# Ten groups of tiles in place of nine, early keys in banks of their own, MLP weights prepared on VectorE, 33 loads, a new order

## The chip, the core and the metric

One core of one Trainium2 chip runs the whole kernel. The metric is device time in microseconds (us), lower is better. The profile shows the engines TensorE (PE; its weight loads PEld), VectorE (DVE), ScalarE (ACT), GpSimd (POOL) and SyncE (SP, which here only issues transfers).

## What is computed

A gated block of cross attention and a small quantised MLP, over 32 blocks ("tiles") of 128 rows by D = 128. S = 128 queries and S2 = 120 keys in each tile, hidden width 512.

```python
def _proj(x, W1, b1, W2, b2):
    h = jnp.einsum('bsd,od->bso', x, W1) + b1
    return jnp.einsum('bsd,od->bso', h, W2) + b2
# attention
qp, kp = _proj(q, W1, b1, W2, b2), _proj(k, W1, b1, W2, b2)
qk = jnp.einsum('bqd,bkd->bqk', qp, kp) * scale + mask
attn = jax.nn.softmax(qk, axis=-1)
attn_out = jnp.einsum('bqk,bkd->bqd', attn, v1)
# MLP: inputs, weights and biases rounded and clipped to 8 bits
h = relu(fixed_quant(einsum('bsi,oi->bso', fq(x), fq(w1)) + fq(b1)))
ffn_out = einsum('bsi,oi->bso', h, fq(w2)) + fq(b2)
# block
x = x + tanh(g_xattn[0]) * attn_out(_layernorm(x), ctx, ctx, mask, ...)
x = x + tanh(g_ffn[0]) * ffn_out(_layernorm(x), ...)
```

## The kernel before

The 32 tiles are cut into nine groups, `TILES = [2, 4, 4, 4, 4, 4, 4, 4, 2]`. Every group g goes through the same stages, each a function of that name on one engine:

- VectorE `stats1` takes mean and variance of x; GpSimd `roots` takes the inverse roots for the batches of groups that `ROOTS` lists; `normalise_pool` and `normalise_dve` share the normalised tiles.
- TensorE `transpose_x`, ScalarE `copy_xT` to SBUF. TensorE `project_keys` multiplies the group's keys by one folded matrix `Mk` (made at the start by `fold_mm1`, `fold_cp1`, `fold_mm2`, `fold_cp2` on TensorE and VectorE), ScalarE `copy_keys`. Then TensorE `scores`.
- VectorE `row_maxima` adds the (negated) mask and takes the maxima, ScalarE `exponentials`, TensorE `transpose_probs`, ScalarE `copy_probsT`, TensorE `attend` (times v), VectorE `residual`.
- VectorE `stats2`, GpSimd `roots`, `quantise_pool` or `quantise_dve`, TensorE `transpose_xq`, ScalarE `copy_xqT`, TensorE `hidden` (four chunks c of 128 hidden units, each in a PSUM bank `bank_H[c]`), `relu` for each chunk on ScalarE (`RELU_ON_ACT` says how many) or VectorE (`relu_dve`), TensorE `mlp_out`, VectorE `result`, and SP stores the group.

The weights of the MLP arrive as load `w`. ScalarE `scale_weights` rounds all 1028 columns of them to 8 bits (`mp_8`, line 528), and makes `w1_q` of them (line 532); GpSimd `widen_weights` makes `w2_q` and the biases. ScalarE also negates the mask (517) and makes a bf16 identity (513). `fold_base` on TensorE, ScalarE `copy_base` and VectorE `split_base` prepare a constant that `mlp_out` adds.

PSUM: `bank_T` takes both the transposed x and the projected keys in turn, so that each waits until ScalarE has copied the other; only group 0's keys go to `bank_H[0]`. SBUF buffers rotate in rings of four (`RING`). `keep_warm` puts matmuls of a zero matrix between the others ("fillers", line 379): 30 at the opening, and then 22, 9, 8, 5 and 5.

Each engine runs its steps in the order of the numbers in the table `DUE` (name and group), and waits on semaphores for its inputs. The 29 entries of `LOADS` are each one transfer on SP, but for the first on ScalarE's queue.

## Time and profile before

| | |
|---|---|
| median of 3 runs | 64.2 us (64.16 to 64.68) |
| profiled execution | 63.99 us, span 61.9 us |
| TensorE clock granted, mean | 0.998 |
| busy: PE / DVE / ACT / POOL | 57.4 / 50.8 / 49.5 / 44.6 us |
| share of the span | 93 / 82 / 80 / 72% |
| transfers | 9.08 MB, mean 147 GB/s |

The span is the time from the first to the last instruction of the profiled execution; its whole time is 2.1 us longer. Busy time is the union of an engine's instructions; a busy TensorE is not at its peak. The chain of waits follows, back from the last instruction, what released each; the timeline lists instructions in order of time, and in brackets how long the engine had been idle before and what it waited for.

### The profile page before, as it was taken

How to read it: one execution, taken by the hardware profiler on the slowest of the kernel's cores; microseconds unless marked ns; L12 is line 12 of the kernel's file. 1: busy time of each engine (PE TensorE's matmuls, PEld its weight loads, DVE VectorE, ACT ScalarE, POOL GpSimd, SP SyncE). 2: the span in 40 equal slices, each digit the busy share in tenths (PEclk: the TensorE clock that was granted, in tenths of full speed). 3: DMA queues.
4: the chain of work that ended last, by engine and by line, in shares of the span. 5: the costliest groups of instructions: out<-in, count | busy, mean ns of one | idle time of the engine just before them, and what ended most of it. 6: DMA issues, size and time to landing. Idle time of an engine off the chain costs nothing.

```text
span 61.9 us, 1729 instructions
## 1 busy us (share of the span) xinstructions
PE 57.4 (93%) x530; PEld 46.1 (74%) x530; DVE 50.8 (82%) x214; ACT 49.5 (80%) x137; POOL 44.6 (72%) x91
## 2 busy tenths in 40 slices
PE   3999999999999999999999999999999999989720
PEld 3999966676897888876987698798978685738310
DVE  4899919988978989979969979989988999973730
ACT  0800288979979899999999999999999896968700
POOL 5968899998989899989899999559339139170000
PEclk9999999999999999999999999999999999999999
DMA  0799999999999500002000400040040040404042
GB/s 0 207 324 345 309 370 396 404 375 386 382 390 376 185 16 5 0 0 85 0 11 0 164 5 0 5 169 11 0 169 0 0 169 11 167 3 169 0 169 85
DMA packets 5482, 9.08 MB, mean 147 GB/s; under 512 B 609, under 2 KB 2658, under 8 KB 5474
## 3 DMA queue, kind: packets, MB, share of 16 engines
q1 hardware_dynamic: 5328, 8.85, 40.2%
q10 hardware_dynamic: 146, 0.13, 0.7%
q8 instruction: 4, 0.07, 0.4%
q14 instruction: 4, 0.03, 0.1%
HBM read 6.88 MB, written 2.10 MB: 145 GB/s over the span
## 4 chain that ended last, share of the span: by engine, by line
PE 82%; POOL 5%; issue 4%; DVE 3%; ACT 1%; POOLq 1%; DVEq 0%
PE bank_A L451 12%; PE bank_S L435 12%; PE bank_O L492 10%; PE bank_T L413 10%; PE bank_H L379 9%; PE bank_H L477 8%; PE bank_A L444 6%; PE bank_T L426 6%; PE bank_O L487 3%; PE bank_H L466 3%; POOL rs L344 3%; POOL xq L362 2%; DVE y_sb L704 2%; ACT pr L559 1%; POOLq L123 1%
## 5 line engine op out<-in xcount | busy, mean ns | idle before, releaser
L344 POOL TENSOR_TENSOR rs<-ve,half 128x4 f32<-128x4 f32 (+2 forms) x17 | 16.6, 979 | 8.7 <-DVE nm L611 6.3
L586 ACT ACTIVATE h<-bank_H,fb_q 128x512 int8<-128x512 f32 (+1 forms) x27 | 16.3, 654 | 1.5 <-PE bank_H L477 1.5
L362 POOL TENSOR_SCALAR xq<-feed_sb,nm,rs 128x128 int8<-128x128 f32 x29 | 12.6, 451 | 0.9 <-POOL rs L344 0.2
L559 ACT ACTIVATE pr<-sc,mn 128x120 f32<-128x120 f32 x32 | 12.3, 400 | 0.2 <-DVE mn L656 0.2
L606 DVE BATCH_NORM_STATS2 st<-feed_sb 128x6 f32<-128x256 f32 x32 | 12.2, 417 | 0.0
L352 POOL TENSOR_SCALAR xn<-feed_sb,nm,rs 128x128 f32<-128x128 f32 x26 | 11.3, 448 | 0.4
L668 DVE SCALAR_TENSOR_TENSOR feed_sb<-bank_A,rec,feed_sb 128x128 f32<-128x128 f32 x32 | 9.1, 345 | 1.9 <-issue 1.7
L435 PEld LDWEIGHTS bank_S<-kpT,xaT 128*128 128x128 f32 x64 | 8.2, 191 | 2.0 <-issue 1.3
L492 PE MATMUL bank_O<-w_q,h 128*128 128x128 bf16 x128 | 9.0, 220 | 0.0
L451 PE MATMUL bank_A<-feed_sb,prT 120*128 120x128 f32 x64 | 8.9, 279 | 0.0
L656 DVE CUSTOM_DVE_ANT_0 sc<-bank_S,mask_neg 128x120 f32<-128x120 f32 x32 | 7.1, 277 | 2.1 <-PE bank_S L435 2.1
L435 PE MATMUL bank_S<-kpT,xaT 128*128 128x120 f32 x64 | 8.7, 276 | 0.0
L704 DVE SCALAR_TENSOR_TENSOR y_sb<-bank_O,tg_out,feed_sb 128x512 f32<-128x512 f32 (+1 forms) x9 | 6.2, 690 | 2.8 <-PE bank_O L492 2.2
L551 ACT ACTIVATE xaT<-bank_T 128x512 f32<-128x512 f32 (+1 forms) x9 | 5.0, 551 | 4.4 <-PE bank_T L426 4.3
L477 PE MATMUL bank_H<-xqT,w_q 128*128 128x512 bf16 (+1 forms) x36 | 8.4, 356 | 0.0
L451 PEld LDWEIGHTS bank_A<-feed_sb,prT 120*128 120x128 f32 x64 | 8.0, 191 | 0.6 <-ACT prT L568 0.4
L492 PEld LDWEIGHTS bank_O<-w_q,h 128*128 128x128 bf16 x128 | 7.2, 98 | 1.2
L379 PE MATMUL bank_H<-zeros_h 128*128 128x128 bf16 x79 | 6.7, 249 | 1.0 <-POOL zeros_h L324 1.0
L413 PE MATMUL bank_T<-feed_sb,Mk 128*128 128x480 f32 (+1 forms) x16 | 7.5, 549 | 0.0
L379 PEld LDWEIGHTS bank_H<-zeros_h 128*128 128x128 bf16 x79 | 6.2, 117 | 1.0 <-POOL zeros_h L324 1.0
L559 ACT ACTIVATION_READ_ACCUMULATOR pr<-sc,mn 128x1 f32 x32 | 6.6, 205 | 0.0
L568 ACT ACTIVATE prT<-bank_A,tg 120x512 f32<-120x512 f32 (+1 forms) x9 | 5.8, 639 | 0.5 <-PE bank_A L444 0.2
...
## 6 DMA issues: line engine op xcount, KB each, us to landing
...
```

Source lines behind the costliest of these rows:

```text
L344: nc.gpsimd.tensor_tensor(rs[:, cols], ve[:, cols], half[:, 0:cols.stop - cols.start], ALU.pow).then_inc(rs_done, 1)
L352: nc.gpsimd.tensor_scalar(xn[g % RING][:, tile(j)], x_of(g, j), nm1[:, of(g, j, 1)], rs[:, root_cols(1, g, j)], ALU.add, ALU.mult).then_in ...
L362: nc.gpsimd.tensor_scalar(low_byte(xq16[g % RING], tile(j)), x_of(g, j), nm2[:, of(g, j, 1)], rs[:, root_cols(2, g, j)], ALU.add, ALU.mult ...
L379: nc.tensor.matmul(bank_H[3][:, 0:P], zeros_h[:, :], zeros_h[:, :], start=True, stop=True)
L413: nc.tensor.matmul(bank_of_keys(g)[:, cols(g, K)], Mk[:, :], fed(f"k{g}"), start=True, stop=True).then_inc(kp_ready, 1)
L435: mm = nc.tensor.matmul(bank_S[:, j * K:(j + 1) * K], xaT[g % RING][:, tile(j)], kpT[g % RING][:, j * K:(j + 1) * K], start=True, stop=True)
L451: mm = nc.tensor.matmul(bank_A[:, tile(j)], prT[g % RING][:, tile(j)], v_of(g, j), start=True, stop=True)
L477: nc.tensor.matmul(bank_H[c][:, cols(g)], w1_q[:, c * P:(c + 1) * P], xqT[g % RING][:, cols(g)], start=True, stop=True).then_inc(h_ready, 1)
L492: mm = nc.tensor.matmul(bank_O[:, tile(j)], h16[g % RING][:, at].bitcast(BF16), w2_q[:, c * D:(c + 1) * D], start=False, stop=(j == TILES[ ...
L559: nc.scalar.activation(pr[i][:, j, :], sc[i][:, j, :], ACT.Exp, scale=-1.0, bias=mn[:, of(g, j, 1)], accum_out=den[:, of(g, j, 1)]).then_i ...
L586: nc.scalar.activation(low_byte(h16[g % RING], hcols(c, g)), bank_H[c][:, cols(g)], ACT.Relu, bias=fb1_q[:, c:c + 1]).then_inc(h_act[c], 1)
L606: nc.vector.bn_stats(both, pair).then_inc(st_done, 1)
```

## The change

- `TILES` becomes `[2, 2, 4, 4, 4, 4, 4, 4, 2, 2]`: ten groups; `ROOTS` has 20 batches for 17, and no batch joins two groups any more.
- Keys of the first four groups go to `bank_H[0]`, `[1]`, `[2]`, `[0]` and no longer share `bank_T` with x (`KEYS_AHEAD = 4`). Keys in SBUF rotate in five buffers, the MLP's three kinds in three.
- The rounding of the weights, `w1_q` and the negated mask move from ScalarE to VectorE; the bf16 identity moves to GpSimd's start; the bias row stays on ScalarE (`round_bias`).
- The shares move: x tiles normalised on VectorE from 6 to 5, quantised there from 3 to 2, hidden chunks from 9 to 12. One 1024-column fill of `h16` less on VectorE.
- Fillers behind the opening: 22, 8, 2, 3 in place of 22, 9, 8, 5, 5. 33 loads for 29, of the same bytes.
- All of `DUE` is new, and so the order on each engine.

```diff
-TILES = [2, 4, 4, 4, 4, 4, 4, 4, 2]
+TILES = [2, 2, 4, 4, 4, 4, 4, 4, 2, 2]
...
+KEY_RING = 5
+MLP_RING = 3
+KEYS_AHEAD = 4
+XN_ON_POOL = [2, 1, 2, 3, 4, 3, 4, 4, 2, 2]
+XQ_ON_POOL = [2, 2, 4, 4, 4, 4, 4, 4, 1, 1]
+RELU_ON_ACT = [2, 3, 3, 2, 3, 3, 3, 3, 3, 3]
+HBYTES_DVE = 1
+LOADS = ['a', 'x0', 'x1', 'x2', 'k0', 'm', 'k1', 'x3', 'k2', 'x4', 'w', 'x5', 'k3', 'v0', 'v1', 'k4', 'x6', 'x9',
+ 'v5', 'x8', 'k5', 'v2', 'v4', 'x7', 'v3', 'v6', 'v9', 'k6', 'v8', 'v7', 'k7', 'k9', 'k8']
...
-FILLERS = [22, 9, 8, 5, 5]
+FILLERS = [22, 8, 2, 3]
...
-            return bank_H[0] if g == 0 else bank_T
+            return bank_H[g % 3] if g < KEYS_AHEAD else bank_T
...
+            pool.wait_ge(ident_up, 1)
+            nc.gpsimd.tensor_copy(ident_h[:, :], ident[:, :]).then_inc(ident_h_up, 1)
...
             def project_keys(g):
-                if g == 0:
-                    pe.wait_ge(fold_cp, 5)
-                else:
+                if g < 3:
+                    pe.wait_ge(fold_cp, 5 if g == 0 else 6)
+                elif g < KEYS_AHEAD:
+                    pe.wait_ge(kp_out, g - 2)
+                if g >= KEYS_AHEAD:
                     pe.wait_ge(xT_out, g)
...
             def transpose_x(g):
                 if g == 0:
                     pe.wait_ge(ident_up, 1)
+                elif g < KEYS_AHEAD:
+                    pe.wait_ge(xT_out, g)
                 else:
                     pe.wait_ge(kp_out, g + 1)
...
-                    pe.wait_ge(kp_out, 1)
+                    pe.wait_ge(kp_out, KEYS_AHEAD)
...
-            def scale_weights():
-
-                wait_block(act, "w")
-                nc.scalar.activation(mp_8[:, :], mp_sb, ACT.Copy, scale=W_SCALE).then_inc(quant8, 1)
+            def round_bias():
                 act.wait_ge(row_in, 16)
...
-                nc.scalar.activation(w1_q[:, :], mp_8[:, 0:C * P], ACT.Copy, scale=1.0 / W_SCALE).then_inc(w1_up, 1)
...
+            def negate_mask():
+                wait_block(dve, "m")
+                nc.vector.tensor_scalar(mask_neg[:, :], mask_sb, -1.0, None, ALU.mult).then_inc(mask_up, 1)
+
+            def round_weights():
+                wait_block(dve, "w")
+                nc.vector.tensor_scalar(mp_8[:, :], mp_sb, W_SCALE, None, ALU.mult).then_inc(quant8, 1)
+
+            def widen_w1():
+                dve.wait_ge(quant8, 1)
+                nc.vector.tensor_scalar(w1_q[:, :], mp_8[:, 0:C * P], 1.0 / W_SCALE, None, ALU.mult).then_inc(w1_up, 1)
```

TensorE at the start, behind the 30 opening fillers. `Wc` is the folded weight in the making, `Mk` in a row's input marks a projection of keys, `ident,xn` a transpose of normalised x, `zeros_h` fillers. Before:

```order
L386 MATMUL bank_H<-feed_sb 128x129
L379 MATMUL bank_H<-zeros_h 128x128 x22
L390 MATMUL bank_H<-Wc 128x128
L391 MATMUL bank_H<-bc,Wc 128x1
L396 MATMUL bank_O<-row_sb,ones 128x2
L426 MATMUL bank_T<-ident,xn 128x128 x2
L379 MATMUL bank_H<-zeros_h 128x128 x9
L413 MATMUL bank_H<-feed_sb,Mk 128x240
L413 MATMUL bank_T<-feed_sb,Mk 128x480
L435 MATMUL bank_S<-kpT,xaT 128x120 x2
L379 MATMUL bank_H<-zeros_h 128x128 x8
```

Now:

```order
L392 MATMUL bank_H<-feed_sb 128x129
L385 MATMUL bank_H<-zeros_h 128x128 x22
L436 MATMUL bank_T<-ident,xn 128x128 x2
L396 MATMUL bank_H<-Wc 128x128
L397 MATMUL bank_H<-bc,Wc 128x1
L385 MATMUL bank_H<-zeros_h 128x128 x8
L421 MATMUL bank_H<-feed_sb,Mk 128x240
L436 MATMUL bank_T<-ident,xn 128x128 x2
L402 MATMUL bank_O<-row_sb,ones 128x2
L421 MATMUL bank_H<-feed_sb,Mk 128x240
L445 MATMUL bank_S<-kpT,xaT 128x120 x2
L436 MATMUL bank_T<-ident,xn 128x128 x4
```

Group 0's transposes (now line 436) stand ahead of the second fold (`Wc`), the gates' matmul (line 402, `row_sb,ones`) behind group 1's transposes, and group 1's keys and tiles are of two instead of four.

VectorE around the row maxima (`sc,mn<-bank_S`) of group 1. Before, from group 0's reciprocal on:

```order
L661 RECIPROCAL rec<-den 128x2
L622 TENSOR_SCALAR xn<-feed_sb,st,rs 128x128 x2
L606 BN_STATS st<-feed_sb 128x6 x2
L609 TENSOR_SCALAR ve<-st 128x4
L611 TENSOR_SCALAR nm<-st 128x4
L656 ISA sc,mn<-bank_S,mask_neg 128x120
L656 ISA mn 128x1
```

Now, from the statistics (`BN_STATS`) of group 4 on:

```order
L603 BN_STATS st<-feed_sb 128x6 x2
L606 TENSOR_SCALAR ve<-st 128x4
L608 TENSOR_SCALAR nm<-st 128x4
L670 RECIPROCAL rec<-den 128x2
L619 TENSOR_SCALAR xn<-feed_sb,st,rs 128x128
L646 TENSOR_SCALAR mp<-feed_sb 128x1028
L665 ISA sc,mn<-bank_S,mask_neg 128x120
L665 ISA mn 128x1
```

The rounding of the weights (line 646) stands directly ahead of group 1's row maxima.

TensorE at the end: `xqT,w_q` is `hidden`, `ident_h,xq` is `transpose_xq`, `base_h,units_h` begins an `mlp_out`. Before, from the output of group 6 on:

```order
L492 MATMUL bank_O<-w_q,h_2 128x128 x16
L477 MATMUL bank_H<-xqT,w_q 128x512 x4
L466 MATMUL bank_H<-ident_h,xq_0 128x128 x2
L487 MATMUL bank_O<-base_h,units_h 128x128 x4
L492 MATMUL bank_O<-w_q,h_3 128x128 x16
L477 MATMUL bank_H<-xqT,w_q 128x256 x4
L487 MATMUL bank_O<-base_h,units_h 128x128 x2
L492 MATMUL bank_O<-w_q,h_0 128x128 x8
```

Now, likewise from the output of group 6 on:

```order
L497 MATMUL bank_O<-base_h,units_h 128x128 x4
L502 MATMUL bank_O<-w_q,h_0 128x128 x16
L476 MATMUL bank_H<-ident_h,xq_2 128x128 x2
L487 MATMUL bank_H<-xqT,w_q 128x256 x4
L497 MATMUL bank_O<-base_h,units_h 128x128 x4
L502 MATMUL bank_O<-w_q,h_1 128x128 x16
L476 MATMUL bank_H<-ident_h,xq_0 128x128 x2
L487 MATMUL bank_H<-xqT,w_q 128x256 x4
L497 MATMUL bank_O<-base_h,units_h 128x128 x2
L502 MATMUL bank_O<-w_q,h_2 128x128 x8
L497 MATMUL bank_O<-base_h,units_h 128x128 x2
L502 MATMUL bank_O<-w_q,h_0 128x128 x8
```

Before, an output of each group stands ahead of the next group's `hidden`; now `hidden` of groups 7, 8 and 9 each stand ahead of the output of the group before.

## Rows read from the trace of the kernel before

**Rows 1.** Chain of waits, one period of a four-tile group: start, length (us), what

```profile
30.61 0.44 PE bank_T L426 x4
31.05 0.89 PE bank_A L451 x8
31.94 0.33 PE bank_O L487 x4
32.27 1.00 PE bank_O L492 x16
33.27 0.86 PE bank_H L477 x4
34.13 0.81 PE bank_T L413 x2
34.94 0.44 PE bank_A L444 x4
35.38 0.89 PE bank_S L435 x8
36.26 0.22 PE bank_H L466 x4
```

**Rows 2.** Chain of waits: the opening, the base, and at 24.58 us

```profile
0.97 3.14 PE bank_H L379 x30
...
4.39 1.23 PE bank_H L379 x22
...
6.09 0.31 PE bank_O L396 x2
...
13.86 0.34 PE bank_O L404 x4
14.20 0.17 PE bank_O L405
...
24.58 0.44 PE bank_A L444 x4
```

**Rows 3.** Busy time by stretch: from:to, us, each engine's busy us (instructions), PEclk, DMA

```profile
4.00:20.00 16.00, 15.91 (x132) 12.53 (x131) 13.49 (x70) 11.54 (x39) 14.36 (x27) 1.00 1.03 370
20.00:50.00 30.00, 30.00 (x280) 24.99 (x278) 27.11 (x122) 29.17 (x84) 23.62 (x44) 1.00 0.12 44
50.00:61.90 11.90, 8.47 (x95) 5.56 (x93) 7.39 (x19) 7.26 (x15) 3.46 (x6) 0.99 0.27 101
```

**Rows 4.** Timeline of TensorE at the end: start, length (us), engine, line, operation

```profile
54.49 1.04 PE L477 MATMUL bank_H<-xqT,w_q 128*128 128x512 bf16 x4
```

**Rows 5.** Timeline of ScalarE at the end

```profile
54.92 1.84 ACT L586 ACTIVATE h<-bank_H,fb_q 128x512 int8<-128x512 f32 x3 [0.48 <-PE bank_H L477]
...
57.59 1.21 ACT L586 ACTIVATE h<-bank_H,fb_q 128x256 int8<-128x256 f32 x3 [0.56 <-PE bank_H L477]
```

**Rows 6.** Timeline of VectorE, first row maxima and last result

```profile
9.27 0.28 DVE L656 CUSTOM_DVE_ANT_0 sc<-bank_S,mask_neg 128x120 f32<-128x120 f32 x1 [1.26 <-PE bank_S L435]
...
59.28 0.48 DVE L704 SCALAR_TENSOR_TENSOR y_sb<-bank_O,tg_out,feed_sb 128x256 f32<-128x256 f32 x1 [0.66 <-PE bank_O L492]
```

**Rows 7.** Groups of instructions by shape: line, operation, count, busy us, mean ns

```profile
L695 DVE TENSOR_SCALAR h<-bank_H,fb_q 128x512 int8<-128x512 f32 x6 | 4.5, 748 | 0.1
...
L600 DVE MEMSET h<- 128x1024 f32 x2 | 1.8, 912 | 0.3 <-issue 0.3
...
L695 DVE TENSOR_SCALAR h<-bank_H,fb_q 128x256 int8<-128x256 f32 x3 | 1.4, 472 | 0.0
...
L528 ACT ACTIVATE mp<-feed_sb 128x1028 int8<-128x1028 f32 x1 | 1.0, 1047 | 0.0
...
L635 DVE TENSOR_SCALAR Wc<-Wc,lift 128x128 f32<-128x128 f32 x1 | 0.3, 287 | 0.0
...
L639 DVE TENSOR_SCALAR Mk<-bank_H 128x128 f32<-128x128 f32 x1 | 0.3, 278 | 0.0
```

**Rows 8.** Timeline of GpSimd, its first root

```profile
4.72 0.74 POOL L344 TENSOR_TENSOR rs<-ve,half 128x2 f32<-128x2 f32 x1 [0.62 <-DVE nm L611]
```

More of the change, by code:

```diff
@@ new lines @@
+    transpose_x=[573, 758, 896, 1133, 1751, 2169, 2593, 3026, 3890, 4317],
+    fold_mm2=[622],
+    project_keys=[727, 811, 1030, 1221, 1458, 1909, 2333, 2736, 3459, 3999],
+    spread_gates=[789],
+    scores=[849, 987, 1345, 1584, 1984, 2395, 2939, 3373, 4031, 4411],
+    transpose_probs=[1082, 1441, 1680, 2087, 2501, 2901, 3305, 3962, 4463, 4780],
+    attend=[1272, 1540, 1821, 2229, 2648, 3069, 3726, 4111, 4624, 4936],
+    fold_base=[1717],
+    transpose_xq=[1789, 2317, 2878, 3344, 3704, 4084, 4485, 4800, 5183, 5418],
@@ new lines @@
+    hidden=[2125, 2545, 3158, 3491, 3816, 4333, 4668, 4980, 5263, 5498],
+    mlp_out=[2788, 3234, 3576, 4199, 4512, 4824, 5055, 5305, 5536, 5675],
+    copy_xT=[652, 833, 1042, 1329, 1820, 2248, 2668, 3308, 3953, 4368],
+    copy_keys=[799, 883, 1199, 1379, 1675, 2090, 2513, 2940, 3578, 4201],
+    gate=[917],
+    round_bias=[949],
+    exponentials=[967, 1254, 1524, 1921, 2333, 2753, 3100, 3801, 4292, 4652],
+    copy_probsT=[1164, 1488, 1748, 2156, 2575, 2994, 3521, 4038, 4567, 4841],
+    copy_xqT=[1869, 2485, 3051, 3415, 3751, 4152, 4602, 4877, 5220, 5454],
@@ new lines @@
+    copy_base=[2072],
+    relu0=[2213, 2632, 3251, 3612, 3981, 4396, 4727, 5032, 5299, 5534],
+    relu1=[2298, 2717, 3358, 3669, 4235, 4453, 4784, 5146, 5370, 5569],
+    relu2=[0, 2904, 3464, 0, 4095, 4510, 4926, 5089, 5334, 5605],
+    stats1=[364, 427, 592, 786, 974, 1258, 1742, 2074, 2879, 2990],
+    fold_cp1=[491],
+    fold_cp2=[688],
+    normalise_dve=[0, 724, 882, 1079, 0, 2170, 0, 0, 0, 0],
+    negate_mask=[749],
+    row_maxima=[934, 1217, 1464, 1889, 2301, 2660, 3057, 3749, 4202, 4574],
@@ new lines @@
+    reciprocals=[1070, 1428, 1881, 2292, 2741, 2942, 3590, 3965, 4614, 4767],
+    round_weights=[1104],
+    residual=[1376, 1615, 1971, 2382, 2775, 3189, 3845, 4242, 4715, 5032],
+    stats2=[1545, 1678, 2196, 2563, 3292, 3493, 4040, 4412, 4779, 5163],
+    widen_w1=[1838],
+    relu_dve3=[2485, 3138, 3388, 3617, 4136, 4508, 4842, 5097, 5332, 5661],
+    relu_dve2=[2524, 0, 0, 3683, 0, 0, 0, 0, 0, 0],
+    split_base=[2749],
+    result=[2951, 3454, 3974, 4346, 4649, 4966, 5226, 5443, 5622, 5756],
@@ new lines @@
+    quantise_dve=[0, 0, 0, 0, 0, 0, 0, 0, 4933, 5371],
+    roots=[445, 609, 731, 926, 1165, 1539, 1639, 1803, 2097, 2379, 2479, 2752, 3025, 3266, 3421, 3703, 4154, 4525, 4860, 5244],
+    normalise_pool=[523, 687, 840, 1036, 1366, 1968, 2207, 2852, 3335, 3985],
+    widen_weights=[1266],
+    quantise_pool=[1717, 1881, 2580, 3094, 3531, 3813, 4263, 4635, 4938, 5322],
+    relu3=[2857, 2858, 2859, 2860, 2861, 2862, 2863, 2864, 2865, 2866],
+    rstd1=[521, 684, 885, 1196, 1437, 1895, 2564, 3076, 3513, 3887],
@@ L94 @@
+    rstd2=[1760, 2310, 2755, 3176, 3606, 3971, 4401, 4886, 5270, 5556],
+    relu_dve0=[2395, 2826, 3344, 3856, 4312, 4708, 5001, 5361, 5669, 5848],
+    relu_dve1=[2431, 2876, 3429, 3970, 4454, 4850, 5085, 5417, 5719, 5883],
+    keep_warm0=[572.5],
+    keep_warm1=[726.5],
+    keep_warm2=[986.5],
+    keep_warm3=[1220.5],
 )
@@ L131, in sem, with ring @@
             return es.enter_context(nc.semaphore(name))
-        def ring(name, shape, dt=F32):
-            return [sb(f"{name}_{i}", shape, dt) for i in range(RING)]
+        def ring(name, shape, dt=F32, n=RING):
+            return [sb(f"{name}_{i}", shape, dt) for i in range(n)]
         feed_sb = sb("feed_sb", list(feed.shape))
@@ L204, in flamingo_gated_block @@
         xaT = ring("xaT", [D, N])
[L205 removed]
+        kpT = ring("kpT", [D, TG * K], n=KEY_RING)
         sc = ring("sc", [P, TG, K])
@@ L491, in mlp_out @@
                         at = slice(c * N + j * D, c * N + (j + 1) * D)
-                        mm = nc.tensor.matmul(bank_O[:, tile(j)], h16[g % RING][:, at].bitcast(BF16),
+                        mm = nc.tensor.matmul(bank_O[:, tile(j)], h16[g % MLP_RING][:, at].bitcast(BF16),
                                               w2_q[:, c * D:(c + 1) * D], start=False,
@@ L596, in _ @@
         def _(dve):
-            for i in range(RING):
+            for i in range(MLP_RING):
                 nc.vector.memset(xq16[i][:, :].bitcast(F32), BYTE_PAIR).then_inc(bytes_up, 1)
```

148 lines of the change are left out of this document (43 added, 105 removed).

## The prediction

> **What bounds the kernel now.** I read the chain of waits first. From 0.97 to 50.48 us it runs almost without a break on TensorE. One group of four tiles costs there what the nine rows of one period say: transposing the normalised x 0.44, attention values 0.89, the MLP's output 0.33 + 1.00, hidden layer 0.86, keys 0.81, transposing the probabilities 0.44, scores 0.89, transposing the quantised x 0.22, together 5.88 us, so 1.47 us for a tile and 47.0 us for 32 [rows 1]. With the 30 opening fillers (0.97 to 4.11), the folds and gates (4.11 to 4.39 and 5.62 to 6.40: 1.06), the base (0.34 + 0.17) and 49 further fillers this is TensorE's whole day [rows 2]. A filler in that second kind is 1.23 / 22 = 56 ns [rows 2], so 49 are 2.74 us.
>
> Count what TensorE had to do by 24.58 us: keys of 22 tiles, scores and x transposes of 18, probabilities and values of 10, two tiles quantised and in the hidden layer come to 14.2 us; with 4.11 for the opening, 1.57 and 2.74 that is 22.7. So about 1.9 us until then are waits [rows 2]. From there to the hidden layer of group 7 at 54.49 [rows 4] only some 0.6 us are: the middle is bound by TensorE's own work. The busy table by stretch says how near the others are: from 20 to 50 us TensorE is busy 30.00 of 30.00, ScalarE 29.17, VectorE 27.11, GpSimd 23.62 [rows 3]. From about 50 on the chain goes through ScalarE and the residue of the last groups: TensorE is busy only 8.47 of 11.90 us [rows 3].
>
> **The change, part by part.** The tiles are the same 32, and a keys or hidden matmul of two tiles costs half of one of four, so the tile work of TensorE stays 47.0 us. What can move is fillers, waits, and the shape of the end.
>
> *Fillers.* 49 become 35: 14 x 56 ns = -0.78 us, if work stands ready in their place.
>
> *Front.* I laid the new rows of each engine one behind the other with the durations of before. VectorE has one 1024-column memset less (912 ns [rows 7]), GpSimd has two as before plus one small cast. GpSimd's first root waited 0.62 us for VectorE's statistics, until 4.72 [rows 8]; these can start about 0.4 earlier, and the root at about 4.4. But its transposes now stand ahead of the second fold on TensorE, which goes from 5.62 to about 6.5, and the folded key matrix is ready at about 7.1, 0.4 later than it was; the first keys start at 7.4, as before. Group 0's scores end near 9.2 (9.13 was before). Row maxima start at 9.6, not 9.27 [rows 6], since VectorE has the mask (0.3) and two normalised tiles ahead of them. Then two-tile group 1 and keys in banks of their own let TensorE run on: scores of group 1 at 10.05, x of group 3 at 11.75, keys of 3 at 12.2, scores of group 2 at 13.5, of 3 at 15.9 (they wait for row maxima of 2, VectorE having had the weights' rounding before), x of 4 at 17.7, a wait of 0.3 for GpSimd's first quantised tiles at 18.3, scores of 4 at 20.15, values of group 3 at 22.4. At that point it has 13.4 us of tile work done, where before had 14.2 at 24.58, so 13.4 at about 23.75. The front gains 23.75 - 22.4 = 1.35 us, 0.78 of it fillers and 0.57 waits. If fillers merely turn into waits it is 0; if no wait were left it would be 0.78 + 1.9 = 2.7; I take the laid-out 1.35.
>
> *Middle.* VectorE gets more. The rounding of the weights, 1028 columns, isn't there before on this engine. ScalarE took 1047 ns for it; VectorE's slope from 256 to 512 columns is (748 - 472) / 256 = 1.08 ns a column, so 472 + 772 x 1.08 = 1.31 us, and its memset of 1024 columns took 0.91: I take 1.2 [rows 7]. Widening w1 (512 columns) is 0.75 by the 512-column row. Twelve hidden chunks instead of nine: +1 of 748 and +2 of 472 = 1.69. One group more costs two statistics tails, a reciprocal and a result, together about 1.0; the mask 0.3; one x tile and one quantised tile less, -0.7. That is +4.2 of work behind the memsets (the smaller of these are estimates from rows of their kind). In the middle stand about 2.3 of it (w1's widening 0.75, one chunk of 512 and one of 256 more, 1.22, and part of the tails). VectorE was idle 30.00 - 27.11 = 2.89 there, so it fits, just. Laid out without a wait, VectorE ends the result of group 4 at 46.8 and TensorE wants it at about 48.9; residuals of 3 and 6 come late by 0.25 and 0.5 for the probabilities' transposes behind them, on which in turn values and MLP queue. ScalarE, the fuller engine, is relieved of its 1047 ns of rounding [rows 7], of w1, the mask and the identity, and takes about 0.8 for a group more. GpSimd gets three root batches, one x tile and one quantised tile more, against 6.38 us of idle time in the middle [rows 3]: nothing. I put +0.4 on the middle over before, for what the laying out leaves unseen; ends 0 and, if 1.8 of VectorE's 2.3 don't fit, +1.8.
>
> *Loads and rings.* 33 loads bring the same bytes as 29. The DMA engines are full from 4 to 20 us (share 1.03 [rows 3]), so four more issues hide in SP's backlog; without that cover they'd cost an issue each. x of group 1 comes at half the size and so earlier. MLP buffers go from four to three: a chunk then waits for the output three groups back, which the order has long before. Both at nothing.
>
> At the weights' rounding a rule bears. The rows show no faster VectorE rate from SBUF than from PSUM: 287 ns for 128 columns SBUF to SBUF against 278 from PSUM [rows 7], and I price by that. The Trainium skill (VectorE: DVE Perf Modes, section Mode 2×_2P) says that a one-source fp32 operation between SBUF tensors can take two elements a cycle, and SBUF — State Buffer, section Who interferes with whom, that meanwhile GpSimd is locked out for the whole instruction. By it the rounding would be an estimated 0.6 us instead of 1.2, and the sum 0.3 lower if the row maxima behind it gain, or the same if GpSimd loses as much.
>
> *End.* Before, from the hidden layer of group 7 (54.49) to the start of the last result (59.28) are 4.79 us [rows 4, 6]. ScalarE starts its three chunks 0.43 behind that (1.84 for three), then copies xqT, then takes three of 256 columns from 57.59 in 1.21 [rows 5]. In the change this point H has groups 6 (output), 7, 8 and 9 behind it. ScalarE: one chunk of group 6 first, group 7's three from H+0.55 to H+2.3, xqT to 2.65. TensorE: hidden 7, output 6 to 2.2, then hidden 8 now stands *ahead* of output 7 and starts at H+2.7, output 7 at 3.15 to 4.5, xqT of 9 to 5.0, hidden 9, output 8 to 6.15, result 8 to 6.65, output 9 (0.17 + the chunks) to 7.4. Last result at H+7.45. Work behind H is 2.54 us more than before (a whole output, two two-tile stages: 1.33 + 1.21), so 4.79 + 2.54 = 7.33: the end costs +0.12; with a late root up to +0.5. It holds less per group but one round trip more.
>
> Sum: -1.35 + 0.4 + 0.12 = -0.83 us. The profiled execution took 63.99 us with a span of 61.9 (2.1 us lie around it), the median is 64.2, 0.2 over it. So the profiled time would be 63.2 and the median **63.4**.
>
> **Rivals.**
> (a) *VectorE takes over as bound; slower.* In favour: it is 90% busy in the middle and gets 2.3 us more; its idle time of before lay partly where its inputs weren't there, and would not all be usable. If the old 2.89 idle stays, the middle grows by 2.3: -1.35 + 2.3 + 0.12 = +1.07, so 65.3. It decides from 1.9 us of growth on to be over 1% slower. Against: its results have slack to TensorE at most of the checkpoints above (46.8 to 48.9). 0.15.
> (b) *The fillers turn into waits and the middle slips a little; no change.* The cover of 14 fillers was 0.78 us in places where row maxima and exponentials were under way; if those are late by as much (they move by +0.3 at 9.6 already), the front gives only the 0.57 and the middle takes 0.4 to 0.6: -0.57 + 0.5 + 0.12 = +0.05, 64.25. 0.33.
> (c) *TensorE's clock falls in the thinner front.* The granted clock is 1.00 up to 50 us, 0.99 behind [rows 3]. The opening's fillers took 3.14 / 30 = 105 ns, the pace of 1.2 GHz, the later ones 56, that of 2.4 GHz [rows 2]: a stretch of 3 us of work at the low level costs about 3 us, 67. Against: in the front TensorE is busy 15.91 of 16.00 [rows 3], and the laid-out waits are under 0.5 each. The Trainium skill (TensorE: Matmul & The Clock Gate, section What's actually happening) has it that throttled is the default state and activity lifts it; fewer fillers go against that. 0.03.
> (d) *It gains more:* no extra wait in the middle and half of the 1.35 us of waits that my front still has gone: -1.35 - 0.67 + 0.12 = -1.9, 62.3. 0.09.
> The forecast itself, 62.9 to 63.8: 0.40.
>
> **Numbers.** 1% (about what a measurement here can tell from no change) is 63.56 and 64.84. Faster: 0.33 of the forecast's 0.40, the 0.09 of (d), and 0.06 of (b), together 0.48. Same: 0.07 of the forecast, 0.26 of (b), 0.03 of (a), 0.36. Slower: 0.12 of (a), 0.03 of (c), 0.01 of (b), 0.16. Range 62.5 to 64.9, which leaves (c), most of (a) and the far end of (d) out.
>
> **What would show it.** In the new profile: first keys at 7.4, row maxima of group 0 at 9.6, values of group 3 at 22.4 (front); VectorE's share near 88% and waits for residuals ahead of probabilities' transposes under 1 us in total (middle); hidden 7 to the last result 7.4 to 7.8 us (end); rounding at 1.2, or 0.6 by the rule with a GpSimd idle of as much beside it; clock 1.00. The prediction is wrong if the x transposes in the front wait for GpSimd, whose roots go from 17 to 20, or if TensorE in 20 to 50 falls under 29 of 30.

## The result

The changed kernel takes 65.14 us (median of 4 runs, 64.98 to 65.18), the kernel before beside it 64.29 (4 runs, 64.16 to 64.68): ratio 1.0144, 95% interval 1.010 to 1.019. It is slower by 1.4%, where 63.4 and a range of 62.5 to 64.9 were forecast. In the five later rounds the kernel before ran 89 times more, from 63.73 to 65.44 with a median of 64.55, so that the change costs some 0.6 us (0.9%) rather than 0.85. A ratio here leaves out runs over 1.5% above the fastest of the same kernel, which for the kernel before cuts off the top of its scatter, so that ratios and medians can differ.

| | before | after |
|---|---|---|
| profiled execution / span | 63.99 / 61.9 us | 65.13 / 63.3 us |
| busy PE / DVE / ACT / POOL | 57.4 / 50.8 / 49.5 / 44.6 us | 57.5 / 52.5 / 47.7 / 47.2 us |
| start of the last result | 59.28 | 60.71 |

The last result starts 1.43 us later and the span is 1.4 us longer, but the profiled time only 1.14: around the span lie 1.8 us, where the kernel before has 2.1 in its profile and 2.0 on average. No run shows why.

Busy time by stretch of the changed kernel, to set beside [rows 3] (from:to, us, busy us of PE, PEld, DVE, ACT, POOL with counts, granted clock, DMA share, GB/s):

```profile
4.00:20.00 16.00, 15.70 (x126) 12.80 (x124) 14.15 (x71) 9.94 (x33) 15.17 (x28) 1.00 1.03 363
20.00:50.00 30.00, 29.64 (x263) 23.90 (x265) 28.14 (x128) 29.01 (x90) 26.41 (x50) 1.00 0.13 47
50.00:61.90 11.90, 9.11 (x106) 6.58 (x106) 7.94 (x21) 7.21 (x16) 2.48 (x5) 1.00 0.27 101
```

GpSimd is the fullest engine next to TensorE from 4 to 20 us, 15.17 of 16. What that means stands in the chain of waits of the changed kernel, ahead of group 3's last transposes (start, length, what):

```profile
4.58 0.73 POOL rs L349
5.31 0.09 issue
5.41 0.88 POOL xn L357 x2
6.28 0.68 POOL rs L349
...
7.06 0.45 POOL xn L357
7.51 0.98 POOL rs L349
...
8.58 0.94 POOL xn L357 x2
9.52 0.98 POOL rs L349
...
10.60 0.59 POOL xn L357 x2
11.19 0.26 issue
11.45 0.96 POOL xn L357
12.42 0.04 issue
12.46 0.44 PE bank_T L436 x2
```

For eight microseconds the end hangs on GpSimd alone: four roots and eight x tiles, one behind the other. In the kernel before the same stretch of the chain lay on TensorE, but for 1.4 us of group 0's row maxima and exponentials (9.13 to 10.52). Two groups of two at the start, where one of two and one of four stood, put one root more ahead of tiles 9 and 10 (four for three): 0.68 us and 0.1 of issue. The third x tile of group 3 took 0.96 us, not 0.45, and the memsets ended at 4.45, not 4.11. No run takes the root out by itself.

The end, on TensorE's timeline and VectorE's (start, length, engine, line, operation, in brackets the idle time before and for what):

```profile
53.40 0.40 PE L497 MATMUL bank_O<-base_h,units_h 64*128 64x128 f16 x4
...
55.37 0.61 PE L487 MATMUL bank_H<-xqT,w_q 128*128 128x256 bf16 x4 [0.46 <-ACT xqT L572]
...
57.88 0.61 PE L487 MATMUL bank_H<-xqT,w_q 128*128 128x256 bf16 x4 [0.47 <-ACT xqT L572]
...
59.84 0.28 PE L497 MATMUL bank_O<-base_h,units_h 64*128 64x128 f16 x2 [0.58 <-DVE y_sb L713]
```

```profile
60.71 0.48 DVE L713 SCALAR_TENSOR_TENSOR y_sb<-bank_O,tg_out,feed_sb 128x256 f32<-128x256 f32 x1 [0.54 <-PE bank_O L502]
```

Three waits of TensorE, 1.5 us, stand behind the hidden layer of group 7. That layer (H) has a record missing in this trace; output 6 starts at 53.40 and follows it by 0.96 where all four records are there (52.45 to 53.41 in the run a_end5), so H = 52.44. Then the parts are:

| part | forecast | measured | from |
|---|---|---|---|
| front | -1.35 | -0.42 | values of group 3 at 23.33, before's equal work at 23.75 |
| middle | +0.4 | +0.91 | what is left of the sum |
| end | +0.12 | +0.94 | 60.71 - 52.44 = 8.27, against 4.79 + 2.54 |
| sum | -0.83 | +1.43 | 60.71 - 59.28 |

### The profile page after: what moved, and what is told of

It is laid out like the page before. It is cut to its first block, busy times and chain, and to the rows that moved or that the text cites. A ratio compares the mean times of both kernels' runs of the same rounds, so it can differ in the third digit from the quotient of the medians.

```text
span 63.3 us, 1752 instructions
## 1 busy us (share of the span) xinstructions
PE 57.5 (91%) x518; PEld 46.3 (73%) x522; DVE 52.5 (83%) x222; ACT 47.7 (75%) x138; POOL 47.2 (74%) x97
## 4 chain that ended last, share of the span: by engine, by line
PE 70%; POOL 11%; DVE 6%; DMA 4%; issue 3%; ACT 1%
PE bank_O L502 13%; PE bank_A L461 11%; PE bank_H L487 10%; PE bank_S L445 10%; PE bank_T L421 6%; PE bank_A L454 6%; POOL xn L357 6%; POOL rs L349 5%; PE bank_O L497 5%; DMA feed_sb<-in_feed 4%; PE bank_T L436 4%; PE bank_H L476 3%; DVE feed_sb L677 2%; DVE y_sb L713 2%; PE bank_H L421 1%
## 5 line engine op out<-in xcount | busy, mean ns | idle before, releaser
L349 POOL TENSOR_TENSOR rs<-ve,half 128x4 f32<-128x4 f32 (+1 forms) x20 | 17.6, 881 | 6.7 <-DVE nm L608 3.8
L583 ACT ACTIVATE h<-bank_H,fb_q 128x512 int8<-128x512 f32 (+1 forms) x28 | 15.9, 609 | 1.5 <-PE bank_H L487 0.8
L367 POOL TENSOR_SCALAR xq<-feed_sb,nm,rs 128x128 int8<-128x128 f32 x30 | 13.2, 453 | 0.9 <-POOL rs L349 0.2
L357 POOL TENSOR_SCALAR xn<-feed_sb,nm,rs 128x128 f32<-128x128 f32 x27 | 12.3, 466 | 0.5
L487 PE MATMUL bank_H<-xqT,w_q 128*128 128x512 bf16 (+1 forms) x36 | 7.7, 332 | 1.2 <-ACT xqT L572 0.9
L704 DVE TENSOR_SCALAR h<-bank_H,fb_q 128x512 int8<-128x512 f32 (+1 forms) x12 | 7.5, 637 | 0.7 <-PE bank_H L487 0.4
L385 PEld LDWEIGHTS bank_H<-zeros_h 128*128 128x128 bf16 x65 | 5.7, 127 | 1.1 <-POOL zeros_h L327 1.0
```

The source lines that it names most:

```text
L349: nc.gpsimd.tensor_tensor(rs[:, cols], ve[:, cols], half[:, 0:cols.stop - cols.start], ALU.pow).then_inc(rs_done, 1)
L357: nc.gpsimd.tensor_scalar(xn[g % RING][:, tile(j)], x_of(g, j), nm1[:, of(g, j, 1)], rs[:, root_cols(1, g, j)], ALU.add, ALU.mult).then_in ...
L367: nc.gpsimd.tensor_scalar(low_byte(xq16[g % MLP_RING], tile(j)), x_of(g, j), nm2[:, of(g, j, 1)], rs[:, root_cols(2, g, j)], ALU.add, ALU. ...
L385: nc.tensor.matmul(bank_H[3][:, 0:P], zeros_h[:, :], zeros_h[:, :], start=True, stop=True)
L487: nc.tensor.matmul(bank_H[c][:, cols(g)], w1_q[:, c * P:(c + 1) * P], xqT[g % MLP_RING][:, cols(g)], start=True, stop=True).then_inc(h_rea ...
L583: nc.scalar.activation(low_byte(h16[g % MLP_RING], hcols(c, g)), bank_H[c][:, cols(g)], ACT.Relu, bias=fb1_q[:, c:c + 1]).then_inc(h_act[c ...
```

## The experiments

"Changed" is 65.1 us in all of them; the kernel before ran beside each, at medians of 64.4 to 64.7, from 63.7 to 65.4. Its scatter is itself a result (below).

### The weights' rounding on VectorE

**a_one_port**

```diff
-tensor_scalar(mp_8, mp_sb, W_SCALE, None, ALU.mult)
+tensor_scalar(mp_8, mp_sb, W_SCALE, 0.0, ALU.mult, ALU.add, accum_out=mp_sum)
```

> The change with one edit: the weights' rounding on VectorE also writes its sum (a form that, by the Trainium skill, SBUF - State Buffer, section Who interferes with whom, has no 2-port mode). In the profile of the change it took 0.71 us for 1028 columns, and beside it GpSimd's third x tile of group 3 took 0.96 us instead of 0.45. Theory (the two engines exclude each other while VectorE runs at the double rate): the rounding goes to about 1.2 us, GpSimd's three tiles to 1.3 from 1.81, so group 3's transposes start 0.5 earlier, while row maxima of group 1 come 0.5 later; time within 0.3 of the change's 65.1. Rival (GpSimd's tile was slow for another reason, a load or the semaphore): the rounding is as slow as that, but the three tiles stay at 1.8; time +0.3 to +0.5.

**a_round_act**: `round_weights` on ScalarE, at the same place of its order.

> The change with one edit: the weights' rounding is back on ScalarE, between its copy of group 2's x and of group 0's probabilities, where ScalarE stood idle for 0.77 us in the change. Theory (the rounding on VectorE costs twice: 0.6 us ahead of row maxima and 0.5 on GpSimd's x tiles): values of group 3 start 0.4 to 0.6 earlier than at 23.3, time 64.6 to 64.8. Rival (the front waits for GpSimd's longer queue of root batches anyhow): GpSimd's tiles at 1.3 but values of group 3 no earlier than 23.1, time 65.0 to 65.2.

In the changed kernel the rounding ran while GpSimd had an x tile of group 3 in hand (VectorE's timeline, then GpSimd's):

```profile
11.47 0.71 DVE L646 TENSOR_SCALAR mp<-feed_sb 128x1028 int8<-128x1028 f32 x1
```

```profile
10.60 1.81 POOL L357 TENSOR_SCALAR xn<-feed_sb,nm,rs 128x128 f32<-128x128 f32 x3
```

1028 columns took 0.71 us, and the third tile 0.96 instead of 0.45. With the accumulating form the rounding took 1.21 us and the three tiles 1.31; with ScalarE doing it, 1.36. So the rule that the prediction weighed (the Trainium skill, VectorE: DVE Perf Modes, Mode 2×_2P, and SBUF — State Buffer, Who interferes with whom) holds here: VectorE is faster, and GpSimd is held up meanwhile, by 0.51 us during the rounding's 0.71. My 1.2 us was the price of the other form. But the times are 65.12 (65.07 to 65.36) and 65.15 (64.73 to 65.41): half a microsecond less on GpSimd is worth nothing by itself, as a_round_act's rival had it. The values of group 3 started at 23.58 and 23.15, since in these profiles TensorE's opening was late instead (scores of group 1 at 10.86 and 10.58, changed 10.30). So two chains of about equal length seem to lead to group 3; a_front and a_best below test it.

### The order of the end

**a_end_tx**

```diff
 transpose_xq=[..., 5183, 5418]  ->  [..., 4990, 5270]
 stats2[9] 5163 -> 5090; quantise_dve[9] 5371 -> 5300
```

> The change with the end reordered: the quantised x of group 8 is transposed ahead of the output of group 6, that of group 9 ahead of the output of 7, and group 9's statistics stand ahead of group 7's last hidden chunk on VectorE. In the change TensorE waits 0.46 and 0.47 us for ScalarE's copy of these transposes, and the end (hidden of 7 to last result) takes 8.11 us where 7.45 was forecast. Theory (that order makes the round trip TensorE to ScalarE to TensorE bare, twice): both waits go, the end takes 7.2 to 7.5, time 64.2 to 64.5. Rival (ScalarE's chunks bound the end, the waits only move to the outputs): the end takes 7.9 to 8.1, time 64.9 to 65.1.

**a_end_out**

```diff
 mlp_out[6..8] 5055, 5305, 5536 -> 4970, 5250, 5490
 result[6, 7]  5226, 5443       -> 5090, 5325
```

> The change with the end in the pattern of the kernel before: the output of each of groups 6, 7 and 8 stands ahead of the next group's hidden layer, and result 6 and 7 on VectorE likewise. Theory (hidden ahead of output is what costs): the output covers ScalarE's copy; hidden 8 and 9 start right behind outputs; the end gets 0.3 to 0.6 shorter, time 64.5 to 64.8. Rival (group 7's hidden is delayed by output 6, 1.3 us, and ScalarE idles for as long): time 65.3 to 65.8.

65.48 (65.44 to 65.56) and 66.16 (65.99 to 66.35), both above what either side had expected. With the transposes earlier the first wait went, but those of group 9 waited 0.24 for ScalarE's chunk and 0.19 for VectorE's quantised tile. With the outputs ahead of the hidden layers, as the kernel before has them, ScalarE once stood idle for 2.4 us, and the end cost 1 us more. "The hidden layer ahead of the output", a step of my walk, is not the fault.

**a_end4**: `TILES = [2, 2, 4, 4, 4, 4, 4, 4, 4]`, entries of group 9 dropped.

> The changed kernel with its last two groups of two tiles merged into one of four (nine groups; loads, roots and rows of the order of group 9 dropped, nothing else moved). TensorE's tile work is the same. If the end lost time to the number of its round trips (three waits of 0.46, 0.47 and 0.58 us for the copy of the quantised tiles and for a result): from the hidden layer of group 7 to the last result less than 8.1 us, and the time 64.7 or less; VectorE and GpSimd also have one group less of small work in the middle. Rival: a last group of four is a longer last chain (output, result and store of four tiles instead of two cost about 0.4 to 1.0 more behind the last hidden layer), and the time is 65.3 to 66.0: then two short groups at the end are worth what they cost.

67.15 (67.13 to 67.51), ratio 1.042. TensorE's timeline:

```profile
55.59 0.39 PE L497 MATMUL bank_O<-base_h,units_h 64*128 64x128 f16 x4 [1.21 <-DVE y_sb L713]
...
57.88 1.04 PE L487 MATMUL bank_H<-xqT,w_q 128*128 128x512 bf16 x4 [0.68 <-ACT xqT L572]
...
61.09 0.39 PE L497 MATMUL bank_O<-base_h,units_h 64*128 64x128 f16 x4 [0.85 <-DVE y_sb L713]
```

The same waits, each longer: in this order (not tuned anew for nine groups) two short groups at the end are worth 2 us.

**a_bank**

```diff
+def bank_of_out(g): return bank_A if g in (7, 9) else bank_O
 # mlp_out and result use bank_of_out(g); mlp_out(g), g >= 7:
-    pe.wait_ge(y_dve, g)
+    pe.wait_ge(x2_done, B)
+    pe.wait_ge(y_dve, g - 1)
```

> The changed kernel with the MLP's output of groups 7 and 9 put in the attention's bank (free once residual 9 is done) and not in bank_O, so that output 9 doesn't wait for result 8 to be read and output 8 not for result 7. In the changed kernel TensorE waits 0.58 us at 59.84 for that, with one bank. If the one bank is a part of what the end took over the forecast: output 9 follows output 8 at once, the last result starts 0.3 to 0.6 us earlier and the time is 64.6 to 64.8. Rival: ScalarE's and VectorE's last hidden chunks (58.20 to 59.4, and VectorE's behind result 8) come as late as the bank does: under 0.15 us of gain, 65.0 to 65.1.

**a_end5**: the same, and `relu_dve3[9]` 5661 -> 5600, which puts that chunk ahead of result 8.

> The changed kernel with outputs 7 and 9 in the attention's bank, and VectorE's last hidden chunk (group 9) ahead of result 8 instead of behind it. With the bank alone output 9 started at once (59.27), but its last two matmuls waited until 60.31 for that chunk (59.78 to 60.27), and the last result came only 0.14 earlier. With the chunk ahead it is done at about 59.1, ScalarE's third at 59.5: the last result starts at 59.8 to 60.0, 7.4 to 7.5 us behind the hidden layer of group 7 (forecast 7.45, changed kernel 8.27), and the time is 64.4 to 64.6. Rival: ScalarE's last chunk or result 8 behind the chunk decides, and it is 60.3 or later: 64.8 to 65.0.

a_bank: 65.08 (65.07 to 65.09), the rival. Output 9 started at 59.27, but its last matmuls waited for VectorE (TensorE's timeline, then VectorE's):

```profile
60.31 0.28 PE L508 MATMUL bank_A<-w_q,h 128*128 128x128 bf16 x2 [0.32 <-DVE h L710]
```

```profile
59.78 0.48 DVE L710 TENSOR_SCALAR h<-bank_H,fb_q 128x256 int8<-128x256 f32 x1
```

a_end5: 64.55 (64.39 to 64.61), the theory's time, if not its checkpoint; VectorE:

```profile
58.54 0.48 DVE L710 TENSOR_SCALAR h<-bank_H,fb_q 128x256 int8<-128x256 f32 x1 [0.44 <-PE bank_H L490]
59.31 0.48 DVE L719 SCALAR_TENSOR_TENSOR y_sb<-bank_O,tg_out,feed_sb 128x256 f32<-128x256 f32 x1 [0.28 <-PE bank_O L508]
60.08 0.48 DVE L719 SCALAR_TENSOR_TENSOR y_sb<-bank_A,tg_out,feed_sb 128x256 f32<-128x256 f32 x1 [0.28 <-PE bank_A L508]
```

60.08 - 52.45 = 7.63 instead of 8.27. One bank and one chunk behind a result cost the end 0.64 together. The bank alone gave 0.14 (H at 52.51, last result at 60.64), since the chunk then decided; the chunk alone was not run.

**b_bank**: the kernel before, with `bank_A` for group 8's output.

> The kernel before with its last output (group 8) in the attention's bank. In its trace TensorE waits 0.41 us at 58.29 for result 7. If the one bank costs the end of before as it costs the changed kernel's: output 8 starts at once behind the hidden layer, the last result 0.2 to 0.3 us earlier after the hidden layer of group 7 (4.5 instead of 4.79), and the time about 0.25 less than before. Rival: ScalarE's third chunk (to 58.75) and VectorE's (58.14 to 58.55, behind result 7) decide: under 0.1 us.

64.70 (12 runs, 63.94 to 65.09), ratio 1.003 (0.998 to 1.008); from H to the last result 4.79 as before. There ScalarE's third chunk ends last (58.83, VectorE's 58.67), so the one bank costs only the changed kernel's end.

### VectorE, ScalarE and the order in the middle

**a_relu3**

```diff
-RELU_ON_ACT = [2, 3, 3, 2, 3, ...]
+RELU_ON_ACT = [2, 3, 3, 3, 3, ...]    # relu2[3] at 3700
```

> The changed kernel with one thing moved: the hidden chunk 2 of group 3 goes from VectorE to ScalarE (three of its chunks there, one on VectorE, as in most groups). In its trace VectorE takes both chunks at 37.73 to 39.1, ahead of group 7's row maxima, and residual 6 ends 0.46 us after TensorE could use it. If VectorE being full there is what the middle lost: the waits around the transposed probabilities of group 7 (41.4 us) fall by 0.3 to 0.46 and the time to 64.7 or 64.8. Rival: ScalarE is as full, and its exponentials of group 7 and copy of the quantised tiles slip by the 0.6 that the chunk takes; then the wait only changes its name: 65.0 to 65.3.

65.23 (65.15 to 65.30). VectorE:

```profile
40.31 1.13 DVE L677 SCALAR_TENSOR_TENSOR feed_sb<-bank_A,rec,feed_sb 128x128 f32<-128x128 f32 x4 [0.99 <-issue]
```

VectorE is now idle for 0.99 us and residual 6 starts when it did (40.28). It waits for the values of group 6, and TensorE, at 41.49, for it.

**a_mid**: a_relu3, and `result[2]` 3974 -> 3800, `mlp_out[3]` 4199 -> 3950.

> The changed kernel with chunk 2 of group 3 on ScalarE, result 2 ahead of residual 6 on VectorE and output 3 ahead of the transposed probabilities of group 7 on TensorE. With the chunk alone on ScalarE nothing moved: VectorE was then idle for 1.0 us and residual 6 still ended at 41.45, because it waits for values 6 (39.1 to 40.05), and only 1.08 us of TensorE's work stands between values 6 and those transposes, where residual 6 needs 1.4. If the order's short cover, and not VectorE's load, is what the middle lost there: the wait of 0.35 us at 41.46 goes, outputs 6 and what follows come 0.2 to 0.35 earlier, 64.8 to 64.9. Rival: the hidden chunks of group 4 on ScalarE (42.74, 44.13) are late for hidden layer 5, which now comes sooner behind the values, and the wait only moves: 65.1 to 65.3.

65.78 (65.56 to 65.82). The wait at the transposed probabilities went, and two came behind it (TensorE); from the values of group 3 to H it is 29.67 us (23.40 to 53.07), 0.56 more than in the changed kernel:

```profile
45.30 0.44 PE L436 MATMUL bank_T<-ident,xn 128*128 128x128 f32 x2 [0.18 <-ACT kpT L541]
...
46.94 0.68 PE L445 MATMUL bank_S<-kpT,xaT 128*128 128x120 f32 x4 [0.24 <-issue]
```

An output of 1.33 us is cover for whoever waits behind it, and moving it bares another pair.

**a_thin_act**, **a_thin_dve**

```diff
+def thin(g, c, chunks): return half the columns if 2 <= g <= 6 and c in chunks else all
 # ScalarE: chunks (1, 2); VectorE: chunks (2, 3)
```

These two leave out half of the conversion in those chunks, to see what the engine's load is worth.

> The changed kernel with a part left out: in groups 2 to 6 ScalarE's hidden chunks 1 and 2 convert only the first half of their columns (nine chunks of about 0.57 us become 0.34, so 2 us of ScalarE's work in the middle are gone; the output's values are wrong for these). TensorE's work and every wait stay as they are. If ScalarE's load (29.0 of 30 us between 20 and 50) is what the middle lost: output 6 starts at 52.6 to 52.9 instead of 53.40 and the time is 64.4 to 64.7. Rival: the round trips of the order (values behind transposed probabilities with one copy between, residual behind values) are what TensorE waits for, not a queue: less than 0.2 us, 64.9 to 65.1.

> The changed kernel with the same part left out on VectorE: in groups 2 to 6 its hidden chunks (six of them) convert only half of their columns, 472 instead of 748 ns each, 1.7 us in all. If VectorE's load is what the middle lost (the rival (a) of the prediction): output 6 starts 0.4 to 0.8 us earlier than 53.40, and the time is 64.4 to 64.7. By the theory of round trips: less than 0.2 us, 64.9 to 65.1.

65.09 (65.01 to 65.19) and 65.31 (65.03 to 65.33). From 20 to 50 us ScalarE's busy time fell from 29.01 to 27.72 and VectorE's from 28.14 to 27.04, and from the values of group 3 to H nothing moved: 29.11 and 29.10 us (23.36 to 52.47; 23.24 to 52.34), as in the changed kernel. Neither of these two engines' load is what the middle lost. GpSimd's was not tried, though it grew most there: 26.41 us of 30, for 23.62 before [rows 3]. Its timeline shows no idle time over 0.2 us from 4.58 to 34.86, and in a_best (below) much of the chain of waits from 27.16 to 49.45 goes through it:

```profile
47.71 1.75 POOL xq L370 x4
49.45 0.41 PE bank_A L457 x2
```

### The opening and the fillers

**b_fill35**: the kernel before with `FILLERS = [22, 8, 2, 3, 0]`.

> The kernel before with the change's number of fillers and nothing else: blocks of 22, 8, 2, 3 and none in place of 22, 9, 8, 5, 5 (35 and not 49). It prices the first term of the sum by itself. As predicted (real work stands ready behind them): 14 x 56 ns go, so 0.8 us less than before, about 63.5 with before at 64.3. Rival: the fillers of the second kind filled waits for VectorE and ScalarE, and what follows them starts when it did: before's time within 0.3 us, with idle time of TensorE in the trace where they stood. A third way, that the clock is granted later with fewer of them: slower than before by up to a microsecond, with the slow pitch of 107 ns in the opening's fillers.

64.84 (10 runs, 63.83 to 65.25), ratio 0.997 (0.991 to 1.003). Fourteen fillers fewer are worth nothing: from the first keys to the last result both traces have 52.11 us. Its chain of waits:

```profile
4.89 1.98 PE bank_H L379 x22
...
10.66 0.87 ACT pr L559 x4
11.52 0.48 ACT xaT L551
12.00 0.95 ACT mp L528
12.95 0.20 ACT fb L530
...
13.57 0.65 ACT kpT L544
14.22 0.04 issue
14.26 0.65 PE bank_T L426 x4
```

Where fillers went, TensorE waits for ScalarE, which has the weights' rounding ahead of a copy of keys. And this execution took 65.04 us: the 22 fillers took 1.98 us, where the profile of before has 1.23 [rows 2]; the second fold starts at 6.71 instead of 5.48, and from the first keys (8.23 for 7.17) to the last result (60.34 for 59.28) everything stands 1.06 later.

**b_fill12**: the kernel before with 12 for 22. **b_fill6**: with 6.

> The kernel before with 12 in place of 22 fillers behind its first fold, nothing else. Its times scatter from 63.7 to 65.2; in the profile of 63.99 these 22 took 1.23 us (56 ns each), in that of b_fill35 (65.04) they ran until 6.7 at about twice the pitch, and all that came behind stood 1.06 us later until the end. If these fillers at the slow pace are on the path of the slower runs: with 12 of them the second fold starts at 5.5 to 6.0 in every run, the highest times fall by 0.5 or more (all within 63.8 to 64.7) and the median is 64.0 to 64.2 with before at 64.4. Rival: the pace rises only with enough work behind it; with 10 fillers fewer it rises as much later, fold and first keys run at the slow pace, and the times are those of before or worse (64.5 to 65.2). Other rival: nothing moves, since VectorE's fold decides: the scatter stays.

> The kernel before with 6 in place of 22 fillers behind its first fold. With 12 its times went from 63.85 to 65.43 down to 63.88 to 64.62, and in that profile the second fold still started at 5.97, right behind the last filler. If the fillers at the slow pace are the whole of it: the second fold follows VectorE's fold at 5.5 in every run, the highest time is 64.3 or less and the median 63.9 to 64.1. Rival: TensorE now idles for some 0.2 to 0.5 us ahead of the fold, its pace rises later, and the first keys and scores run at half pace (their rows at twice the length): 64.5 or more.

| kernel | runs | from | median | to |
|---|---|---|---|---|
| before, beside b_fill12 | 23 | 63.85 | 64.72 | 65.43 |
| b_fill12 | 12 | 63.88 | 64.20 | 64.62 |
| before, beside b_fill6 and a_best | 23 | 63.79 | 64.61 | 65.44 |
| b_fill6 | 12 | 63.76 | 64.31 | 64.41, but for two at 67.27 and 67.53 |

Ratios 0.997 (0.993 to 1.0004) and 0.999 (0.995 to 1.003). The upper half of the scatter of the kernel before is the block of 22 at a late pace: with 12 its upper 0.8 us is gone, and 0.7 stays. TensorE in b_fill12 and, behind it, in b_fill6:

```profile
4.69 1.49 PE L379 MATMUL bank_H<-zeros_h 128*128 128x128 bf16 x12
5.97 0.54 PE L390 MATMUL bank_H<-Wc 128*128 128x128 f32 x2
```

```profile
5.87 0.49 PE L390 MATMUL bank_H<-Wc 128*128 128x128 f32 x2 [0.35 <-DVE Wc L635]
```

With 12 the theory's times came out. With 6 the second fold waits for VectorE and starts at 5.87, 0.1 earlier than with 12 and not at 5.5, and two of twelve runs lost some 3 us. No trace of such a run was taken, and that the pace rose much later in them is a guess.

**a_fill12**: the changed kernel with 12 for 22.

> The changed kernel with 12 in place of 22 fillers ahead of group 0's transposes of x. In its trace they end at 6.19 us with the transposes right behind them, and in three other runs of its kin at 6.5 to 6.8, since TensorE's pace rose later than in before's trace (where 22 took 1.23). If this block is on the path and its slow pace is a part of what the front lost: the transposes start at 5.6 to 5.9, the first keys at 7.0 or a little under, values of group 3 some 0.3 us earlier, and the whole is 64.8 to 64.9 (changed kernel 65.1). Rival: what decides is GpSimd's first normalised tiles and VectorE's fold behind them, so nothing before 7.3 moves and the time stays within 0.1 of 65.1. Other rival: TensorE's pace rises later still with fewer fillers, and the fold and the first keys run at half pace: 65.5 or more.

65.20 (65.19 to 65.30): the first rival. The transposes start at 6.00 instead of 6.19, the first keys at 7.31 as before, the values of group 3 at 23.32, behind the same GpSimd chain.

**a_front**

```diff
-XN_ON_POOL = [2, 1, 2, 3, ...]    HBYTES_DVE = 1
+XN_ON_POOL = [2, 1, 2, 2, ...]    HBYTES_DVE = 2
```

> The changed kernel with GpSimd relieved ahead of 12.5 us: one of its two 1024-column memsets goes to VectorE (two there, as before the change), and one of its three x tiles of group 3 too. In the changed kernel's trace the chain that ends last runs through GpSimd alone from 4.58 to 12.42 us (four roots, eight x tiles) and TensorE waits for its last tile; the split of the first groups put one root more into it (0.71 + 0.1). If that chain is what bounds the front: TensorE's transposes of group 3 don't wait, values of group 3 start near 22.9 instead of 23.33, and the time is 64.7, wherever TensorE's pace rises early; where it rises late, up to 0.4 more, so that the times scatter as those of the kernel before do. Rival: VectorE pays for it (0.9 and 0.35 us more ahead of the row maxima and first statistics), the values of group 3 stay at 23.3 or come later, and the time is 65.1 to 65.6.

65.04 (10 runs, 64.56 to 65.34), ratio 1.012. GpSimd is off the chain and TensorE's transposes of group 3 run through:

```profile
6.61 0.39 PE L436 MATMUL bank_T<-ident,xn 128*128 128x128 f32 x2
...
12.19 0.60 PE L436 MATMUL bank_T<-ident,xn 128*128 128x128 f32 x4
...
23.22 1.16 PE L461 MATMUL bank_A<-feed_sb,prT 120*128 120x128 f32 x8
```

But its 22 fillers ended at 6.61, and the values are at 23.22. Its best run is 0.4 under the changed kernel's, and it scatters over 0.8 us, where the changed one's four runs lie between 65.0 and 65.2. That fits both halves of the theory: with GpSimd's chain gone the front follows the opening's pace, and in the changed kernel whichever of the two is later.

### All together

**a_best**: a_front, 12 fillers, a_end5, and `attend[6]` 3726 -> 3550 with `transpose_xq[4]` 3704 -> 3560 (both ahead of output 2).

> The changed kernel with the single findings put together: one memset and one x tile of group 3 from GpSimd to VectorE, 12 for 22 fillers in the opening, values of group 6 and the transposes of the quantised group 4 ahead of output 2, outputs 7 and 9 in the attention's bank, and VectorE's last chunk ahead of result 8. If each is what I take it for and they add up: values of group 3 at 22.8 to 23.0 (changed kernel 23.33), no wait of TensorE at the transposed probabilities of group 7 (0.36), the last result 7.6 us behind the hidden layer of group 7: 65.1 - 0.4 - 0.35 - 0.55 = 63.8, and 63.6 to 64.1 with the opening's scatter; the kernel before 64.5. Rival: the waits stand in for one another, as ScalarE's and VectorE's did: then only the end's 0.55 remains, 64.5.

63.89 (12 runs, 63.78 to 64.76). TensorE, then VectorE's last result in the chain:

```profile
5.89 0.67 PE L439 MATMUL bank_T<-ident,xn 128*128 128x128 f32 x2 [0.32 <-POOL xn L360]
...
22.77 1.16 PE L464 MATMUL bank_A<-feed_sb,prT 120*128 120x128 f32 x8
```

```profile
59.38 0.48 DVE y_sb L719
```

59.38 is 1.33 earlier than the changed kernel: front 0.56, end 0.65 (7.62 for 8.27), middle 0.12 (28.99 for 29.11), where I had expected 0.35. In the front 12 fillers alone had moved the values of group 3 by 0.01 and a_front alone by 0.11, and its other edits all stand later, so there the two bounds did hide each other. It is 1.2 us under the changed kernel, which ran in another round. Against the kernel before the medians say 0.7 faster, but the ratio is 1.0003 (0.995 to 1.006), and the lowest times are 63.78 and 63.79. So it is no faster at its best, and less often late; that it beats the kernel before in every sense isn't shown.

## Why the prediction was wrong

*What bounds the kernel* held for the middle. For the front it didn't: I took the 1.9 us until 24.58 as waits that a better order could use, and never asked on whom they hung. In b_fill35, where fillers went, two of them hang on ScalarE's chain (0.22 us at 10.51 and 0.25 at 14.26); for the rest no run says on whom they hang.

*Fillers, -0.78* (part of the front's -1.35). Failed where it was tested: in the order of the kernel before they are worth 0 (b_fill35), since no work stood ready behind them. This is what rival (b) named. In the new order no run adds them back.

*Front, -1.35.* The step that failed most, -0.42. The walk holds up to the scores of group 1 (10.05 forecast, 10.30) and the first transposes of group 3 (11.75; 11.85). Then keys of 3 come at 12.90 (12.2), scores of 2 at 14.21 (13.5), of 3 at 16.69 (15.9), values of 3 at 23.33 (22.4). Most of the 0.7 (keys of 3 come at 12.35 in a_best) arises at GpSimd, to which the prediction gave "nothing" by its idle 6.38 us in the middle, though the front has 1.64 of 16 us idle [rows 3] and TensorE waits there for the last x tile of group 3, at 12.46. The roots went from 17 to 20, and the "what would make the prediction wrong" named it. With GpSimd's chain and the late fillers both out of the way the same walk gives 22.77 (a_best), so 0.56 of the 0.93 missing are these two and 0.37 the walk.

*The profile that I read from* was an early one among the executions of the kernel before: its 22 fillers at 56 ns were one outcome of several, and its 63.99 lies 0.56 under the median of the 89 later runs. The changed kernel's walk started from it, and the measured column of the table above is counted from it.

*Rounding, 1.2 us.* 0.71; the rule was right, and its lock hit a tile on the chain. It cost nothing in the end, as the opening's pace was the next bound.

*Middle, +0.4.* +0.91. Rival (a) comes near the time (65.3 for 65.14), but by luck: VectorE is busier by 1.03 us of 30 [rows 3], but taking 1.1 us from it does nothing (a_thin_dve), nor does taking 1.3 from ScalarE (a_thin_act). One wait of 0.36 is order: residual 6 needs 1.4 us behind values 6, and 1.08 stand there. Moving it freed 0.12. The rest of the 0.91 is in waits of 0.1 to 0.2 at single rows and stays open; GpSimd, to which the prediction gave "nothing", gained 2.79 us of work there and is an untested rival.

*End, +0.12.* +0.94. The order of events was as walked, its round trips were too short: from a transpose of the quantised tiles to their hidden layer I had 0.5 us, twice (2.2 to 2.7, 4.5 to 5.0), and it is 0.74 (54.63 to 55.37, 57.14 to 57.88); hidden layer 9 and output 8 take 1.39 (57.88 to 59.27), not 1.15. That is 0.72 of 0.82. The 0.64 that a_end5 gets back is another matter: the walk had taken output 9 and VectorE's chunk behind result 8 as given. From the forecast -0.83 to the measured +1.43 it is 2.26: front 0.93, middle 0.51, end 0.82.

*Clock, rival (c).* The granted clock stayed at 1.00, and still the pace of the fillers decided the front of the kernel before.
